# Edge-count one-hots written as 25 rows of 24 with a gap, in a four-layer graph network on one core

## What is computed

```python
edge_index = stack([src, dst])
x = layernorm(x + L0(x, edge_index, edge_type_16))   # sum over edges, a weight by edge type, 2 bases
x = layernorm(x + L1(x, src, dst, edge_type_32))     # twice: sum over edges, 32 types, 4 bases, tanh
x = layernorm(x + L2(x, edge_index))                 # relu((sum over edges of x[src]) @ W.T + b)
x = layernorm(x + L3(x, src, dst))                   # attention over the edges of a node, 8 heads
```

## Time and profile before

| what | us |
|---|---|
| median of three runs | 2035.03 (2030.83 to 2042.31) |
| the profiled execution's own time | 2034.92 |
| its span, first to last instruction | 2033.1 |
| layer 0, with what comes ahead of it | 0 to 547 |
| layer 1 | 547 to 977 |
| layer 2 and what prepares the attention | 977 to 1467 |
| attention | 1467 to 2033 |

### The profile page before, as it was taken

One profiled execution on the slowest core, in us unless ns is written; L12 is line 12 of the kernel. 1 busy time (PEld: TensorE's weight loads), 2 busy tenths in 40 slices (PEclk: granted clock), 3 DMA queues, 4 the chain that ended last, 5 costly groups with the idle time before them and its releaser, 6 DMA issues.

```text
span 2033.1 us, 36067 instructions
## 1 busy us (share of the span) xinstructions
PE 1605.6 (79%) x10129; PEld 1323.2 (65%) x10160; DVE 1505.2 (74%) x4756; ACT 1070.8 (53%) x2202; POOL 1448.6 (71%) x1482
## 2 busy tenths in 40 slices
PE   3878888888589898898489999997728777777777
PEld 2666677666478777787377877774407666566666
DVE  7866666666668888787467877777859877777776
ACT  3355546555587677666465655552464343434341
POOL 6777777777577777776577777772277777777772
PEclk9666566665689999899699999999855555555555
DMA  6232232323133333433533433432286555555551
GB/s 182 56 87 70 74 89 57 87 58 87 51 102 98 103 105 100 134 102 87 147 83 103 139 120 119 125 109 92 81 221 174 163 166 157 165 156 162 160 145 46
DMA packets 171435, 231.75 MB, mean 114 GB/s; under 512 B 48220, under 2 KB 123983, under 8 KB 170980
## 3 DMA queue, kind: packets, MB, share of 16 engines
q0 software_dynamic: 53376, 123.02, 21.9%
q1 hardware_dynamic: 116710, 104.76, 17.4%
q10 hardware_dynamic: 1154, 1.67, 0.3%
HBM read 196.52 MB, written 36.08 MB: 114 GB/s over the span
## 4 chain that ended last, share of the span: by engine, by line
POOL 21%; PE 18%; issue 8%; DVE 5%; DMA 3%; ACT 2%; SPq 1%; DVEq 0%; POOLq 0%; ACTq 0%
POOL G L2004 18%; PE p_d L858 4%; PE p_d L929 4%; PE p_g L916 3%; POOL G L739 3%; PE p_g L806 3%; DMA G<-kv_d,idx 1%; DMA G<-h_d,idx 1%; PE p_o L839 1%; PE p_w L2064 1%; SPq L685 1%; PE p_o L843 1%; ACT agg L1200 1%; DVE hs L2264 0%; DVE PV L2317 0%
## 5 line engine op out<-in xcount | busy, mean ns | idle before, releaser
L739 POOL DMA_INDIRECT G<-h_d,idx x624 | 624.2, 1000 | 218.5 <-issue 177.7
L2004 POOL DMA_INDIRECT G<-kv_d,idx x416 | 406.4, 977 | 162.7 <-issue 159.7
L739 POOL DMA_INDIRECT G<-in_x,idx x416 | 403.4, 970 | 131.6 <-issue 106.4
L806 PEld LDWEIGHTS p_g<-S,G 128*128 128x128 f32 x2080 | 350.5, 231 | 181.0 <-issue 107.0
L806 PE MATMUL p_g<-S,G 128*128 128x96 f32 (+1 forms) x2080 | 373.0, 313 | 116.9 <-DMA G<-in_x,idx 71.0
L1387 DVE SCALAR_TENSOR_TENSOR S<-con,rel,shared 128x96 f32<-128x96 f32 (+1 forms) x1040 | 261.0, 292 | 0.4
L1414 DVE TENSOR_TENSOR agg<-agg,p_g 128x96 f32 (+1 forms) x520 | 119.5, 230 | 190.8 <-PE p_g L806 175.3
L1167 ACT ACTIVATE work<-con,lo_f 128x128 bf16<-128x128 f32 x416 | 143.2, 392 | 221.2 <-PE p_d L818 221.0
L1505 DVE TENSOR_TENSOR work<-work,p_d 128x312 f32 (+1 forms) x416 | 180.7, 464 | 84.1 <-PE p_d L818 78.3
L929 PE MATMUL p_d<-Sb,kv_s 128*128 128x288 f32 x728 | 221.1, 421 | 19.3 <-ACT kv_s L1159 13.7
L2064 PE MATMUL p_w<-oh,PV 128*128 128x40 f32 x832 | 195.1, 410 | 23.9 <-DVE PV L2317 22.8
(11 more groups left out here) (324 smaller groups left out, 2940.8 us busy)
## 6 DMA issues: line engine op xcount, KB each, us to landing
dst_b<-in_dst_row SPq DMA_DIRECT2D x104, 240.0 KB, 3.2
work<-A_d SPq DMA_DIRECT2D x25, 800.0 KB
A_d<-work SPq DMA_DIRECT2D x12, 1600.0 KB, 7.6
G<-h_d,idx POOLq DMA_INDIRECT x624
G<-in_x,idx POOLq DMA_INDIRECT x416
kv_s<-low_d SPq DMA_DIRECT2D x52, 128.0 KB
G<-kv_d,idx POOLq DMA_INDIRECT x416
kv_s<-low_d SPq DMA_DIRECT2D x52, 96.0 KB
```

Source lines behind the costliest of these rows:

```text
L739: pool.indirect_dma_start(G[:, n % GRING, :], None, l.table, bass.IndirectOffsetOnAxis(ap=l.places[:, c:c + 1], axis=0)).then_inc(s_arr[i ...
L806: last = pe.matmul(p_g[:, g % PB, 0:width], G[:, c % GRING, :], S[:, c % (SRING * GR), 0:width], start=(k == 0), stop=(k == GR - 1))
L2004: pool.indirect_dma_start(G[:, c % KRING, :], None, d["kv"], bass.IndirectOffsetOnAxis(ap=idx[:, c:c + 1], axis=0)).then_inc(s_arr[c // QC ...
```

## The change

The 600 numbers of a one-hot are written as 25 rows of 24 with one unused number behind each row, so that a slot of `keys` has 625 numbers in place of 600. What is read, `iota_h`, is the same 600 numbers in one run; in the built program the instruction reads one run of 600 and writes 25 rows of 24 at a pitch of 25. The product's moving operand, 13 or 12 rows of `keys`, is 13 or 12 rows of 24 at a pitch of 25 in place of one run. `work` grows by 200 bytes per partition, and `lows` moves back by as much. No instruction is added, removed or moved on any engine.

```diff
 KEYS = NT * W
+KROW = W + 1
+KEYP = NT * KROW
@@
-    work = sb("work", [P, NT * SLAB // 2 + OHS * (KEYS + P) // 2])
+    work = sb("work", [P, NT * SLAB // 2 + OHS * (KEYP + P) // 2])
@@
-    w_2 = w_1 + OHS * KEYS // 2
+    w_2 = w_1 + OHS * KEYP // 2
@@
-    keys = work[:, w_1:w_2].bitcast(BF16).rearrange("p (c n) -> p c n", c=OHS)
+    keys = work[:, w_1:w_2].bitcast(BF16).rearrange("p (c t w) -> p c t w", c=OHS, w=KROW)[:, :, :, 0:W]
@@ counts
-                last = pe.matmul(p_d[:, 1 + half, 0:(hi - lo) * W], lows[:, slot, :], keys[:, slot, lo * W:hi * W],
+                last = pe.matmul(p_d[:, 1 + half, 0:(hi - lo) * W], lows[:, slot, :], keys[:, slot, lo:hi, :],
@@ one_hots
-            dve.tensor_scalar(keys[:, slot, :], iota_h[:], key_f[:, c:c + 1], None, ALU.is_equal).then_inc(s_hot, 1)
+            dve.tensor_scalar(keys[:, slot], iota_h[:].rearrange("p (t w) -> p t w", w=W), key_f[:, c:c + 1], None, ALU.is_equal).then_inc(s_hot, 1)
```

## The result

The changed kernel takes 2023.87 us (median of 12 runs, 2016.05 to 2029.3). The kernel before, run beside it, takes 2037.44 us (12 runs, 2030.83 to 2042.31). The ratio is 0.9936 with the interval [0.9924, 0.9948]: faster by 13.6 us between the medians, 0.6%. The profiled execution of the changed kernel took 2023.76 us, with a span of 2021.9, 11.2 us less than the span before.

What follows compares the result with a forecast made beforehand. POOL's own pace through the gathers was taken to bound layers 0 and 1. The terms -2.5 (layer 0), -11.2 and +2.5 (layer 1) gave -11.2 us from 2034.9, so 2024 us, with an 8-in-10 range of 2015 to 2041.

Steps and rivals of the forecast that it cites:

- Duration: One-hots on VectorE, layers 0 and 1: from 369 to 522 ns, 32 us more VectorE work in each layer.
- no change of mode: Rival: one-hots still take four columns a beat, 369 ns, collisions stay, time 2035 us; chance 0.10.
- one column a beat at odd places: Rival: one-hots in slots 1 and 3 run at 835 ns, time 2048 us; chance 0.07.
- No hold: Layers 0 and 1: the slower one-hots no longer stretch any gather on POOL, taken from rows with one SBUF input.
- longer and still shuts POOL out: Rival: one-hots at two columns a beat still hold gathers, with more and longer collisions, time 2051 us; chance 0.05.
- Size of the gain in the gathers: Gathers get shorter by 2.5 us in layer 0 and by 11.2 of 13.0 us in layer 1.
- what I had taken off place by place: Layer 1: behind an L1422 only the one-hot's part of a hold goes, leaving 11.2 of 13.0 us.
- The cost to the consumers: Layer 1: slower catching up after its start, about 2.43 us a group, costs 2.5 us (bounds 0 and 19).
- The rival that has the consumers as the bound: Layer 1's consumers take 2.57 us a group, using up POOL's gain; time 2032 to 2041, say 2038 us; chance 0.13.
- the cover: Layer 1, 605 to 681 us: 6.5 us more VectorE work fits in its 7.0 us of waiting for PE.
- The rest: Layer 2 and the attention have none of the changed instructions: 0 us.
- The signs that I had named: Profile after: one-hots about 520 ns, none ending a gather's excess, layer 1's last gather some 13 us earlier, next pass 11.

Runs made afterwards that it cites:

- wide_one_run: Kernel before, with one-hots reading 600 fp32 numbers of a weight in place of the fp16 run, output in one run; counts wrong; ratio 1.0217.
- after: The changed kernel itself, as profiled after the change, against the kernel before; median 2023.87 us, ratio 0.9936.
- after_again: The changed kernel, unaltered, run and traced once more on another chip against the kernel before; ratio 0.9936.
- pitch_26: The changed kernel with two unused numbers behind each row in place of one, so all rows begin at even places; ratio 0.9934 to the kernel before.
- source_gapped: Kernel before, with the gaps in what a one-hot reads (25 rows of 24) and its output still one run of 600; ratio 0.9931.
- before_again: The kernel before, unaltered, run and traced once more on another chip as the baseline there; no time of its own is given.
- one_input: The changed kernel with block factors (L1424) leaving out the weights, so one SBUF input; block sums unweighted; ratio 0.9854 to the kernel before.
- count_psum: The changed kernel with the column numbers that L1389 and L1424 compare with in PSUM, transposed tiles moved to another bank; ratio 0.9951 to the kernel before.
- count_psum_late: The changed kernel with those column numbers in PSUM, and ScalarE copying each transposed tile two slots later than in count_psum; ratio 0.9883 to the kernel before.

## Why the prediction was right, step by step

The time was forecast at 2024 us and came out at 2023.87. The mechanism is shown; the terms are off by a few us each and make up for one another. That the two times agree to 0.2 us is luck: I counted 11.2 us from 2034.9, and the kernel before came out at 2037.44 beside the changed one, so that the gain is 13.6 us by the medians (11.2 in the profiled pair). The range, 2015 to 2041, holds the kernel before too, so that the time lies in it shows little.

**Duration: right.** 522 ns was forecast from L1376's and L1387's rates, 521 measured. The rivals "no change of mode" (369) and "one column a beat at odd places" (835) are out, the second one also by the pitch of 26.

**No hold: right.** That was taken from rows with one SBUF input at one column a beat and not shown by any row of the kernel before. In the trace after no gather of layer 1 has an excess that ends with a one-hot, where 43 had; in layer 0 two do, by 13 ns each. The rival "longer and still shuts POOL out" was run as wide_one_run. By that run its price is some 2.2%, near 2080 us (2035 x 1.0217, an estimate), and not my 2051.

**Size of the gain in the gathers: a little too high.** Layer 0 gave 403.4 - 401.8 = 1.6 us for the 2.5 forecast, layer 1 318.3 - 308.9 = 9.4 for 11.2. In layer 1 the one-hots' 13.0 us are gone and L1387's part fell from 3.2 to 1.7 us, but L1422's (now L1424's) rose from 5.9 to 11.5, with 63 gathers in place of 41. Of that rise, 1.8 us are what I had taken off place by place, where an L1422 stands just ahead of a one-hot; the rest are gathers that meet an L1424 at other places. I take it that this is because every gather behind a removed hold comes earlier, but no run shows that. It isn't chance: L1424's part is 11.5 to 17.9 us in the four kernels whose fp16 one-hots don't hold (after, after_again, pitch_26, source_gapped) and 5.4 to 5.9 in the three with one run. So part of a hold that is taken away comes back as another's, and the sum had no term for it. On the other chip layer 1 gave 12.1 us, so a term of this sort is known to some 3 us from one trace.

**The cost to the consumers: not seen in the time.** I had put 2.5 us on layer 1 for slower catching up. From 605 to 681 us the new trace has this busy time (columns of the earlier trace rows):

```profile
605.00:681.00 76.00, 71.40 (x498) 61.78 (x497) 72.26 (x223) 60.13 (x122) 58.01 (x60) 0.98 0.35 93
```

VectorE's wait for the counts' product in those 76 us, and under it the same in layer 1 as a whole (in total, times, longest):

```profile
DVE work L1507 <- PE p_d L820: 2.7, 4, 1.3
...
DVE work L1507 <- PE p_d L820: 27.6, 20, 4.9
```

DVE is busy 4.6 us more in those 76 us, and its wait for the counts' product fell by 4.3, from 7.0 to 2.7. In all of layer 1 that wait fell from 58.4 to 27.6 us: 30.8 us, nearly the whole of the 32 us that one-hots grew by. So the cover was what I had named. Catching up didn't get slower: VectorE adds 33 groups to the sums in those 76 us in both kernels. The rival that has the consumers as the bound also had a wrong number: it set 2.57 us a group against "POOL's pace today", but that is 413.1 / 156 = 2.65 us, and 2.58 was the pace forecast for the changed kernel (2.59 measured, 403.8 / 156). The way from layer 1's last gather to the next pass even fell, from 16.6 to 13.8 us. That part isn't the change's to keep: on the other chip it was 17.3 before and 17.6 after. The stretch of that way in the kernel before (columns as in the earlier trace rows):

```profile
961.00:977.00 16.00, 8.91 (x44) 7.07 (x43) 5.70 (x21) 0.84 (x3) 0.00 (x0) 0.71 0.61 166
```

The same in before_again:

```profile
963.30:980.60 17.30, 11.38 (x52) 8.79 (x52) 5.71 (x21) 2.08 (x7) 0.03 (x2) 0.70 0.58 158
```

In the changed kernel:

```profile
950.00:964.00 14.00, 6.70 (x47) 5.23 (x45) 6.33 (x24) 1.11 (x5) 0.17 (x2) 0.98 0.73 199
```

And in after_again:

```profile
949.80:967.40 17.60, 11.02 (x73) 8.86 (x73) 10.62 (x36) 2.09 (x7) 0.01 (x1) 0.95 0.59 159
```

TensorE's granted clock is 0.71 and 0.70 there with the kernel before, 0.98 and 0.95 with the changed one. The chain of work that ended last goes through the last two tiles' products; in the kernel before (start us, us, what):

```profile
967.45 1.74 PE p_o L839 x8
...
970.80 2.05 PE p_o L839 x8
```

And in the changed kernel:

```profile
949.07 5.34 DMA G<-h_d,idx
...
955.74 1.16 PE p_o L841 x8
...
958.00 1.13 PE p_o L841 x8
```

Eight products take 1.16 and 1.13 us there after the change, in place of 1.74 and 2.05, and the last gather lands in 5.34 us in place of 6.38. Of the 2.8 us that this way got shorter in this pair, 1.5 are the products and 1.0 the landing. The second pair, with much the same clocks, doesn't have it: there PE is still busy for 11.0 us of the way, in place of 6.7, so its consumers were further behind. VectorE is busy for 10.6 us of it, in place of 5.7 in before_again, and pitch_26 looks like after_again (10.6 us in a way of 17.4). So a cost of the kind that I had put down may be there, some 5 us of work left over, and be paid by the higher clock. What raised the clock isn't shown, and no run separates the two.

**The rest.** Layer 2 and the attention have none of these instructions and were put at 0; in this pair they took 2.3 us more (gathers 307.0 in place of 305.9, and 1.2 us in the rest). The sum of the span: -1.5 until layer 1's first gather, -9.3 in layer 1's series, -2.8 on the way, +2.3 behind, which is -11.3 for the 11.2 measured, the difference being rounding. The forecast -11.2 was -2.5 - 11.2 + 2.5. That the two agree to 0.1 us is luck, and the agreement of the mechanism isn't. The signs that I had named came out in the other order: layer 1's last gather begins 10.7 us earlier, where I had said some 13, and the next pass 13.5 earlier, where I had said 11.

## What to carry to other kernels

Where GpSimd issues transfers one after another and never waits, its pace is the kernel's, and the first thing to look for is which VectorE instruction's end fits the ends of its long ones. A VectorE instruction that is 40% longer but leaves GpSimd alone can be the faster one, as long as VectorE has waits to put the length into; look those waits up first. And look at holding instructions that lie in a row: a run can keep a gather until the last of them ends (12 of 55 times in layer 1 of the kernel before, 35 of 74 with the fp32 source), so that a longer link can cost more than its own length. A hold that is taken away can also come back in part as another instruction's.

## What the runs showed of the hardware

- What holds a gather is not the rate. At about 525 ns a one-hot holds when source and destination are both one run (fp32 source, 528 ns, layer 1's excess 61.3 us) and doesn't when one side is 25 rows (fp16 source, 521 ns, 14.4 us). With the fp32 source and one side in 25 rows, at 835 ns, no one-hot holds either.
- An instruction with two SBUF inputs holds gathers, and the same one with one of them in PSUM doesn't: layer 1's gathers went from 990 ns in the changed kernel (995 on the second chip) to 949 and 948. The Trainium skill says so ("SBUF — State Buffer", section "Who interferes with whom": two SBUF inputs contend with a GpSimd instruction that reads SBUF, one at most doesn't outside the modes that use two ports), and the traces of one_input (956 ns) and count_psum (949) agree. The input from PSUM cost nothing: L1424 takes 511 ns on average in the changed kernel, and 508 in count_psum_late.
- A gather holds a one-hot off in its later part only. In layers 0 and 1 of the kernel before, 45 one-hots that begin within a gather, nearly all 0.50 to 0.70 us after its start, are longer by over 40 ns, and every one of them ends 0.135 to 0.143 us after the gather does (251.18 against 251.04 in the earlier trace rows). Another 75, which begin by 0.47 us and end within a gather of plain length, take 373 ns at most. The Trainium skill ("SBUF — State Buffer", section "Who interferes with whom") has the first comer hold the shared ports for its whole instruction while the other blocks. To the gather's end these traces agree, from its start they don't, as here:

```profile
34.46 0.94 POOL L739 DMA_INDIRECT G<-in_x,idx  x1 [0.30 <-issue]
...
34.88 0.37 DVE L1491 TENSOR_SCALAR work<-iota_h,key_f 128x600 bf16<-128x600 f16 x1
```

- Two bytes off a multiple of four cost these VectorE instructions next to nothing, at two columns a beat (pitch of 25 against 26: 522 and 521 ns) and at four (376 and 377 ns in the slots at odd places, 372 and 374 in the others).
